# Transposing probability tiles two in a row in a causal attention layer on one core

## The reference, cut to what matters

```
q = proj(Wq, bq) * scale;  k = proj(Wk, bk);  v = proj(Wv, bv)
q = apply_rotary(pos, q);  k = apply_rotary(pos, k)
sim = jnp.einsum('bhid,bhjd->bhij', q, k)
sim = jnp.where(causal, -jnp.finfo(sim.dtype).max, sim)
attn = jax.nn.softmax(sim, axis=-1)
out = jnp.einsum('bhij,bhjd->bhid', attn, v)
out = out.transpose(0, 2, 1, 3).reshape(b, n, INNER)
return out @ Wo + bo
```

## Time and profile before

| what | value |
| --- | --- |
| runs | 2095.52, 2101.58, 2101.20 us; median 2101.2 |
| the profiled execution | 2098.68 us |
| its span on the core | 2096.9 us |
| granted TensorE clock over the span | 0.987 |
| TensorE busy | 2031.3 us, 97% |
| GpSimd, VectorE, ScalarE busy | 1617.6, 1388.1, 1377.5 us |

### The profile page before, as it was taken

One profiled execution on the slowest core, in us unless ns is written; L12 is line 12 of the kernel. 1 busy time (PEld: TensorE's weight loads), 2 busy tenths in 40 slices (PEclk: granted clock), 3 DMA queues, 4 the chain that ended last, 5 costly groups with the idle time before them and its releaser, 6 DMA issues. The chain is left out here.

```text
span 2096.9 us, 39596 instructions
## 1 busy us (share of the span) xinstructions
PE 2031.3 (97%) x12616; PEld 1804.4 (86%) x12624; DVE 1388.1 (66%) x2907; ACT 1377.5 (66%) x3070; POOL 1617.6 (77%) x1304
## 2 busy tenths in 40 slices
PE   5999999999999999999999999999999999979997
PEld 5888898888888888888888888888988888868886
DVE  3666676667666666666667666666666666656776
ACT  4677766667776677766667766667666667644543
POOL 5888888888888888788888888788888888724554
PEclk8999999999999999999999999999999999989999
DMA  3433333233332333342333333433332232420000
GB/s 114 122 76 72 77 76 81 71 105 98 76 78 69 79 77 71 98 115 71 73 76 75 76 77 72 116 86 77 77 81 71 72 77 70 111 61 11 21 21 31
DMA packets 109882, 160.30 MB, mean 76 GB/s; under 512 B 31856, under 2 KB 44656, under 8 KB 108272
## 3 DMA queue, kind: packets, MB, share of 16 engines
q1 hardware_dynamic: 86000, 115.82, 22.7%
q10 hardware_dynamic: 23680, 41.95, 7.3%
HBM read 81.95 MB, written 8.65 MB: 43 GB/s over the span
## 5 line engine op out<-in xcount | busy, mean ns | idle before, releaser
L608 ACT ACTIVATE prob<-prob,neg_max 128x128 f32<-128x128 f32 (+7 forms) x512 | 397.3, 776 | 384.3 <-DVE neg_max L739 384.1
L660 DVE TENSOR_TENSOR PT<-TP,PT 128x512 fp32r<-128x512 f32 (+3 forms) x768 | 422.4, 554 | 317.8 <-ACT PT L451 314.2
L451 ACT ACTIVATE PT<-TP 128x512 fp32r<-128x512 f32 (+3 forms) x768 | 359.2, 485 | 182.6 <-PE TP L902 179.7
L739 DVE CUSTOM_DVE_ANT_0 prob<-S,mask_row 128x128 f32<-128x128 f32 (+7 forms) x512 | 381.2, 745 | 39.8 <-PE TP L902 35.7
L386 POOL TENSOR_TENSOR swap<-swap,sin_t 128x512 f32<-128x512 f32 x256 | 333.9, 1304 | 68.5 <-DMA swap<-proj 66.6
L390 POOL TENSOR_TENSOR rot<-rot,swap 128x512 f32<-128x512 f32 x256 | 361.5, 1412 | 21.3 <-DVE rot L770 1.4
L902 PE MATMUL TP<-ident,prob 128*128 128x128 f32 x2304 | 372.0, 275 | 2.3 <-ACT prob L608 2.3
L902 PEld LDWEIGHTS TP<-ident,prob 128*128 128x128 f32 x2304 | 281.9, 141 | 57.5 <-ACT prob L608 2.8
L892 PE MATMUL S<-QKA 128*128 128x512 f32 (+4 forms) x1152 | 261.1, 353 | 2.9 <-ACT proj L616 2.6
L892 PE MATMUL S<-QKB 128*128 128x512 f32 (+4 forms) x1152 | 260.9, 353 | 1.3 <-DVE resid L763 1.3
L376 POOL TENSOR_TENSOR norm_o<-norm_o,bias_o_m 128x512 f32<-128x512 f32 x128 | 134.3, 1049 | 121.6 <-ACT OTA L546 82.0
(11 more groups left out here) (102 smaller groups left out, 3973.8 us busy)
## 6 DMA issues: line engine op xcount, KB each, us to landing
swap<-proj SPq DMA_DIRECT2D x512, 128.0 KB, 2.3
recip_b<-recip_d SPq DMA_DIRECT2D x128, 256.0 KB, 3.9
w_raw<-in_w_heads ACTq DMA_DIRECT2D x64, 256.0 KB, 4.1
wv_raw<-in_w_heads ACTq DMA_DIRECT2D x32, 256.0 KB, 4.4
wo_raw<-in_wo_heads ACTq DMA_DIRECT2D x32, 256.0 KB, 3.5
attn_d<-resid ACTq DMA_DIRECT2D x4, 1024.0 KB, 4.6
x_raw<-in_x_cols SPq DMA_DIRECT2D x3, 1024.0 KB, 8.4
resid<-in_x_rows ACTq DMA_DIRECT2D x3, 1024.0 KB, 5.6
```

Of the source, the lines that this page charges most:

```text
L451: copy = lambda o, i: nc.scalar.activation(o, i, ACT.Copy)
L608: nc.scalar.activation(row, row, ACT.Exp, bias=neg_max[:, s:s + 1], scale=-1.0, accum_out=row_sum[:, s:s + 1]).then_inc(exped, 1)
L660: sub = lambda o, a, b: nc.vector.tensor_tensor(o, a, b, ALU.subtract)
L739: nc.vector.tensor_tensor_reduce(row_view(prob[g][:, prob_at[g][i]:prob_at[g][i] + cols], s), score_view(S[s % 2], s), row_view(mask_row[: ...
```

## The change

Only TensorE's program is changed; the instructions are the same, in another order. In steps 1 to 3 the second transpose of the step goes ahead of the second product. The transposes k = 8 and 9 both stand in step 4, and k = 10 and 11 both in step 6, behind the product k = 9; the products k = 8, 9, 10 stay in the steps 5, 6, 7.

```
@@ -989,8 +989,8 @@
                     elif prev and s < 4:
                         attend(n, 2 * s - 2, nxt, before)
                         transposes(2 * s)
+                        transposes(2 * s + 1)
                         attend(n, 2 * s - 1, nxt, before)
-                        transposes(2 * s + 1)
@@ -999,11 +999,14 @@
                     if s == 4 and prev:
                         attend(n, 6, nxt, before)
                         attend(n, 7, nxt, before)
-                    if s >= 4 and own:
-                        transposes(s + 4)
                     if s > 4 and i is not None:
                         values(i)
-                    if s > 4 and own:
+                    if s == 6 and own:
+                        attend(n, 9, par, vb)
+                    if s in (4, 6) and own:
+                        transposes(s + 4)
+                        transposes(s + 5)
+                    if s in (5, 7) and own:
                         attend(n, s + 3, par, vb)
```

## The result

Over 22 runs the changed kernel has a median of 2102.45 us (2095.58 to 2105.11) and the kernel before, over 22 runs, 2098.27 us (2092.12 to 2101.93). The ratio is 1.0019, interval [1.0011, 1.0028]: 4.0 us slower, 2.3 to 5.9. The kernel is slower beyond the interval; over 22 runs the interval is some 0.1% to each side, finer than the 0.3% that the prediction took for the least that can be told.

A forecast was written before the change was run, and what follows sets the result against it. TensorE, busy 2031.3 of 2096.9 us, was taken as bound; 0 for breaks, 0 for steps 1 to 4 and 3.4 for step 6 gave 2102.1 (profiled execution) or 2104.6 (median); forecast 2103.5 us, range 2093 to 2113.

The forecast's parts named there:

- The cost of a break: Five breaks per head between transposes and other TensorE work go; each was taken to be worth 0.
- bound of a gain of 0.09: Upper bound per removed break, in us, reading the longer first matmul behind a transpose as the break's own price.
- Steps 1 to 3: Second transpose ahead of the second product: the wait for the same split stays in place, cost 0.
- step 4: Transposes 8 and 9 ahead of the scores of step 5: those end 0.33 us later, hidden with 0.3 us of cover.
- Step 6: Product 9, then transposes 10 and 11, ahead of the scores of step 7: 3.4 us more in all.
- late copy of tile 10: ScalarE's copy after transpose 10, starting near 997.87 instead of 997.33: hidden by 0.1 to 0.2 us, then by 0.37.
- T11 ahead of the scores: Transpose 11, one tile, ahead of the scores of step 7: 0.11 us in each of 31 even heads, 3.4 us.
- idle time ahead of A0: TensorE's idle time before the weight load of step 0's attention product in even heads: near 0.51 us instead of 0.40.
- only odd heads count: Delayed step 7 scores of odd heads reach the next even head; those of even heads meet 1.40 us of cover.
- The second rival: Nothing reaches the attention product of step 0, through hidden slack or time given back: 2100 us, chance 0.16.
- The scale: Sum 2102.1 us on the profiled execution's scale, 2104.6 on the median's; the middle, 2103.5, was given.
- The clock: Longer transpose blocks put at 0; its rival had a dip per pair of heads, 52 us more, 2155.5 us, chance 0.04.

The follow-up runs named there:

- the first experiment: Kernel before with only the second transpose in steps 1 to 3 moved ahead of the second product; ratio 0.9998 [0.9987, 1.0008] against the kernel before.

## Why the prediction was right

**The cost of a break, put at 0**, was right to within 0.014 us: the first experiment's 0.11 a tile and its ratio of 0.9998 bear it out. The bound of a gain of 0.09, from the longer first matmul behind a turn, shows how such a row misleads. PEld's timeline of the kernel before, at the product A1 behind four turns:

```profile
1006.87 0.19 PEld L917 LDWEIGHTS O<-PT,VA 128*128 128x128 f32 x1
1006.98 0.19 PEld L918 LDWEIGHTS O<-PT,VA 128*128 128x128 f32 x1
```

The first load starts 0.02 us ahead of its matmul (1006.89), the second 0.23 ahead of its own (1007.21). So the first matmul's load is exposed, as the prediction read it, and the load of a turn in the same place would be as well.

**Steps 1 to 3 and step 4 at 0** were right within the noise, each by a run of its own (0.9998 both).

**Step 6.** The late copy of tile 10 was reckoned to start 0.54 later and started 0.53 later; it was covered. T11 ahead of the scores was the whole loss, reckoned at 3.4 us, measured 3.4 alone (1.0016) and 4.0 in the full change (1.0019), with 3.1 by the length of the pairs. The idle time ahead of A0 was foretold as 0.51 and is 0.51. That only odd heads count was foretold and shown. One sign was put loosely: the scores of step 7 were to be 0.11 later, and it is their end that is (0.12), not their start (0.03).

**The second rival**, that nothing reaches A0, falls with the interval of the result, 2.3 to 5.9 us, and with the longer wait at A0.

**The scale** was the weaker part. The median of three runs, 2101.2, was 2.9 us over that of 22, and I put my number between it and the profiled execution; 2103.5 against a measured 2102.45. The step itself came out, and the choice of scale was worth nearly as much as the change: on the median of the 22 runs the same sum gives 2101.7. So the number's distance of 1 us from the measured one is in part luck, and the evidence for the mechanism is the step, not the number.

**The clock** was put at 0, and no block of turns lowered it. Windows of the changed kernel over two blocks of eight turns and over the heads from 100 to 1800 us:

```profile
1004.60:1005.41 0.81, 0.81 (x10) 1.00 0.00 0
1008.29:1009.10 0.81, 0.81 (x9) 1.00 0.29 66
100.00:1800.00 1700.00, 1687.43 (x10696) 1.00 0.33 80
```

The granted clock is 1.00, 2.4 GHz, in both blocks and on average over the heads. A single dip would not show in that average. Cut into stretches of 3 us, it has one dip, to 0.50 (1.2 GHz) from 1381 us on, where the kernel before has two, to 0.60 from 460 us on and to 0.63 from 1378 on; the rival wanted one in every pair of heads.

The Trainium skill, "TensorE: Matmul & The Clock Gate", Part 4, says that a transpose doesn't count as work for the clock as a matmul does. With blocks of at most eight turns between dense matmuls no effect of it is seen; no run here has turns alone, so the statement itself isn't tested.

## What to carry to other kernels

On an engine that is busy throughout, moving work is not free even when nothing is added: ask which dependent chain through the other engines starts at each instruction and where it comes back, and count what now stands ahead of the chain's start instead of inside it. Work between the start of such a chain and its return is cover; work ahead of the start only delays it. Where an idle time recurs at one place, follow it back to the instruction on the bound engine that starts it and issue that one earlier; here issuing the scores of step 7 earlier in the kernel before gained 6 us, where one turn put ahead of them lost 3 to 4. The whole change with the scores early was not run.

## What the runs showed that I had not expected

A wait can move without its sum changing: with the scores of step 7 1.44 us later, the weight loads of TensorE stood idle 0.41 us ahead of T0 and 1.39 ahead of A0, two places on the same chain, 1.40 in all over the 0.40 of before, and the pair of heads is 1.40 longer. The row of A0's wait alone would have given 0.99 us and a wrong price.

The idle time ahead of a weight load is more than what its matmuls lose. A0's load idled 0.40 us, of which 0.24 was reckoned as lost; with that idle time gone, in the run with the scores early in odd heads, the median pair of heads is 0.22 us shorter.
